# Second chunk's hidden states and first two weight blocks loaded before the last stores of the first phase; its first in-projection ahead of scan unit 0

## The reference, cut to what matters

```python
def _direction(x_bdl, conv_w, conv_b, xproj_w, dtproj_w, dtproj_b, A_log, Dv):
    xc = lax.conv_general_dilated(x_bdl, conv_w, (1,), [(D_CONV - 1, 0)], ...)   # 4 taps, per channel
    xc = (xc + conv_b[None, :, None]).transpose(0, 2, 1)
    x_dbl = xc @ xproj_w.T
    dt = x_dbl[..., :DT_RANK] @ dtproj_w.T + dtproj_b
    Bm = x_dbl[..., DT_RANK:DT_RANK + D_STATE]
    Cm = x_dbl[..., DT_RANK + D_STATE:]
    xc = jnp.clip(xc, -10.0, 10.0)
    dt = jnp.clip(dt, 1e-05, 1.0)
    delta = jax.nn.softplus(dt + dtproj_b)
    A = -jnp.exp(A_log)
    return _selective_scan(xc, delta, A, Bm, Cm, Dv)   # h = exp(delta*A)*h + delta*u*B; y = sum over 16 states of C*h
xz = (hidden_states @ in_proj_w.T).transpose(0, 2, 1)
x, z = jnp.split(xz, 2, axis=1)                        # 2048 channels each
y_fwd = _direction(x, ...)
y_bwd = _direction(x[:, :, ::-1], ...)[:, ::-1, :]
y = (y_fwd + y_bwd) * jax.nn.silu(z.transpose(0, 2, 1))
out = y @ out_proj_w.T
```

## Time and profile before

| | us |
|---|---|
| median of 3 runs | 8235.12 |
| lowest and highest | 8234.53, 8238.75 |
| the profiled execution, whole | 8231.93 |
| its span, first to last instruction | 8230.1 |

### The profile page before, as it was taken

How to read it: one execution, slowest core, us unless ns; L and a number is a source line. 1 busy time by engine, 2 the same in 40 slices (tenths; PEclk the granted TensorE clock), 3 DMA queues, 4 the chain that set the end, 5 groups by cost and what they waited for, 6 DMA issues and landing times. The chain is left out here.

```text
span 8230.1 us, 114768 instructions
## 1 busy us (share of the span) xinstructions
PE 7136.7 (87%) x32512; PEld 4393.1 (53%) x32512; DVE 7156.1 (87%) x7788; ACT 5349.8 (65%) x12640; POOL 6715.8 (82%) x2320
## 2 busy tenths in 40 slices
PE   6578888888888888877899999999999988789999
PEld 3344555555555555554555555555555555534444
DVE  6913999999999999999999999999999999934443
ACT  6634777777777777777777777777777777610000
POOL 5513999999999999999999999999999999821110
PEclk8789999999999999998999999999999999889999
DMA  3363232323232323221323232323233332153442
GB/s 103 90 191 128 70 118 66 118 70 118 67 118 68 119 67 118 68 98 44 113 79 128 76 128 77 131 79 126 89 116 104 104 107 70 63 191 133 136 140 76
DMA packets 557719, 844.05 MB, mean 103 GB/s; under 512 B 129472, under 2 KB 276928, under 8 KB 539712
## 3 DMA queue, kind: packets, MB, share of 16 engines
q1 hardware_dynamic: 557120, 837.10, 31.1%
HBM read 583.89 MB, written 253.02 MB: 102 GB/s over the span
## 5 line engine op out<-in xcount | busy, mean ns | idle before, releaser
L1192 POOL TENSOR_TENSOR scan_w<-scan_du,scan_bcast_b 128x2048 f32<-128x2048 f32 x1023 | 4623.9, 4544 | 45.0 <-DVE scan_h L1239 6.6
L1239 DVE TENSOR_TENSOR_SCAN scan_h<-scan_da,scan_state,scan_w 128x512 f32<-128x512 f32 x2560 | 3185.3, 1276 | 44.2 <-ACT scan_da L1094 27.7
L1094 ACT ACTIVATE scan_da<-scan_delta,scan_prm 128x512 f32<-128x512 f32 x4096 | 2803.1, 685 | 0.0
L973 PE MATMUL scan_yT<-all_ident,scan_hc 128*128 128x128 f32 x10240 | 1540.1, 281 | 660.4 <-DVE scan_hc L1249 659.6
L1239 DVE TENSOR_TENSOR_SCAN scan_hs<-scan_da,scan_state,scan_w 128x512 f32<-128x512 f32 x1536 | 1891.9, 1258 | 45.2 <-ACT scan_da L1094 44.7
L973 PEld LDWEIGHTS scan_yT<-all_ident,scan_hc 128*128 128x128 f32 x10240 | 1175.3, 143 | 1395.5 <-DVE scan_hc L1249 1047.1
L846 PE MATMUL scan_in_ps<-scan_hn,scan_win 128*128 128x512 f32 x3840 | 1732.3, 594 | 13.6 <-issue 13.6
L1249 DVE TENSOR_TENSOR scan_hc<-scan_h,scan_bcast_c 128x512 f32<-128x512 f32 x2560 | 1637.3, 671 | 2.1 <-ACT scan_state L1074 0.7
L1202 POOL TENSOR_TENSOR scan_hp<-scan_hs,scan_bcast_c 128x1024 f32<-128x1024 f32 x512 | 1209.3, 2362 | 49.9 <-DVE scan_hs L1239 42.9
L846 PEld LDWEIGHTS scan_in_ps<-scan_hn,scan_win 128*128 128x128 f32 x3840 | 693.6, 191 | 715.6 <-issue 715.6
L1074 ACT ACTIVATE scan_state<-scan_h 128x1 f32<-128x1 f32 x2560 | 429.5, 168 | 982.8 <-DVE scan_h L1239 977.0
(11 more groups left out here) (122 smaller groups left out, 6918.3 us busy)
## 6 DMA issues: line engine op xcount, KB each, us to landing
yT<-scan_y_out SPq DMA_DIRECT2D x257, 256.0 KB, 2.0
scan_win<-winx SPq DMA_DIRECT2D x128, 512.0 KB, 3.7
xc<-scan_xc_out SPq DMA_DIRECT2D x256, 256.0 KB, 2.0
scan_xc<-xc SPq DMA_DIRECT2D x256, 256.0 KB, 4.1
scan_bcast_b<-bc SPq DMA_DIRECT2D x64, 1024.0 KB, 8.0
scan_bcast_c<-bc SPq DMA_DIRECT2D x64, 1024.0 KB, 8.2
scan_win<-winz SPq DMA_DIRECT2D x128, 512.0 KB, 4.6
scan_x<-x_pad SPq DMA_DIRECT2D x128, 257.5 KB, 2.6
```

The costliest lines, as they stand in the source:

```text
L973: last = nc.tensor.matmul(yT[:, tb], hc_slot(b, n)[:, tb * P:(tb + 1) * P], ident[:], is_transpose=True, start=(i == 0 and tb == 0), stop= ...
L1094: nc.scalar.activation(da[:, n % 2], delta[:, s], ACT.Exp, scale=decay(b, n)).then_inc(S["exp_done"], 1)
L1192: nc.gpsimd.tensor_tensor(w[:, g], du[:].unsqueeze(1).to_broadcast([P, G, T]), bcast_b[:, g * G:(g + 1) * G], ALU.mult).then_inc(S["w_done ...
L1239: nc.vector.tensor_tensor_scan(flip(b, h_slot(b, n)), flip(b, da[:, n % 2]), flip(b, w[:, n // G, n % G]), state_of(b, n), ALU.mult, ALU.a ...
```

## The change

Three things are moved. In SP's order, `load_win(16)`, `load_hn(1)` and `load_win(17)` leave `between` and stand in the last pair of `before_scan`, behind a hold for the last in-projection matmul of the first chunk and in front of the stores of blocks 14 and 15. On PE both halves of the in-projection of block 16 stand in front of unit 0, behind `dt_matmul(0)`, and on ACT its copy stands there too, behind `delta_step(0)`. In unit 0, block 16 has only its convolution and projection left (states 5 and 8), block 17 is projected in at states 0 and 2 instead of 8 and 10, copied at 7 instead of 11, and convolved at 9 instead of 11. The first `turn` of unit 0 moves from state 6 to 8 and its copy and addition to where they are in all units.

```diff
         NORMAL = dict(into=(0, 2), diag=1, copy=7, conv=5, xc=10, proj=11)
-        EARLY = dict(into=(0, 2), diag=1, copy=5, conv=5, xc=8, proj=8)
+        EARLY = dict(into=(), diag=1, copy=NS, conv=5, xc=8, proj=8)
         TURN = dict(diag=1, conv=2, xc=7, proj=8)
-        LATER = dict(into=(8, 10), diag=6, copy=11, conv=11, xc=12, proj=13)
+        LATER = dict(into=(0, 2), diag=6, copy=7, conv=9, xc=12, proj=13)
...
         def turn_steps(b):
-            if b == 0:
-                return dict(mm=(6, 12), copy=(10, NS - 1), add=(12, NS - 1))
             return dict(mm=(8, 12), copy=(12, NS - 1), add=(12, NS - 1))
...
                 store_bc(0)
-                for a in range(2):
-                    load_win(DB + a)
                 hold(sp, S["bc_stored"], LOAD, S["passed"])
                 for c, g in ((0, 0), (0, 1), (1, 0)):
                     broadcast(0, c, g)
-                load_hn(1)
                 load_c_columns(0)
...
                         load_win(a + 2)
+                if j == DB // 2 - 1:
+                    hold(sp, S["in_mm"], DB, S["passed"])
+                    load_win(DB)
+                    load_hn(1)
+                    load_win(DB + 1)
                 for a in (j * 2, j * 2 + 1):
                     before_scan(a)
             between()
...
                 pe.wait_ge(S["scan_done"], b * NS + TN[k] + 1 + SCR)
-                pe.wait_ge(S["in_copied"], (in_copies(b) if b or k else DB + 1) + 2)
+                pe.wait_ge(S["in_copied"], in_copies(b) + 2)
...
                     pe.wait_ge(S["in_copied"], i + 2)
-                    if b or i > DB:
-                        pe.wait_ge(S["h_turn_copied"], b * NTN if b else 1)
+                    if b:
+                        pe.wait_ge(S["h_turn_copied"], b * NTN)
                     in_proj(i % 2, 0, KT // 2)
...
             dt_matmul(0)
+            in_step(DB, 0, 0)
+            in_step(DB, 1, 0)
             for b in range(NU):
                 unit(b)
...
             delta_step(0)
+            act.wait_ge(a_in[DB % 2], (DB // 2 + 1) * (NA * LOAD))
+            in_copy(DB)
             for b in range(NU):
                 unit(b)
```

## The result

| | before | after |
|---|---|---|
| median of 11 runs each, us | 8234.53 | 8216.05 |
| lowest and highest | 8222.72, 8238.75 | 8209.94, 8224.22 |
| ratio, 95% interval | | 0.9982 (0.9974 to 0.9989) |
| profiled execution, whole | 8231.93 | 8214.63 |
| its span | 8230.1 | 8212.9 |

The change gains 18.5 us by the medians, with an interval of 9 to 21 us. The forecast was 15 us, 8220 for the median.

The account below looks back on a forecast made before the run. DVE was taken to bound the units, POOL close behind. Start -6.6, unit 0's idle time +21.0 and unit 1 +0.5 made 15 us, 8235.1 to 8220; forecast 8216.5 to 8224 (0.60), 8 in 10 within 8212 to 8228.

Parts of the forecast that it names:

- rival 1: Last stores of chunk 0 are not held up by the loads; gain 19 us, 8216 us; chance 0.20.
- The store of xc 14 behind the loads: On SP's queue, this store waits for the 3.4 MB asked for ahead; delay 3.8 us (2.3 to 5).
- Columns of C in time: At the start of unit 0, columns arrive near 736, ACT needs them near 738; the 5.04 us wait goes.
- In-projection 16 ahead of unit 0: On PE, 16 matmuls starting at half clock put the first scan at P0 + 12.0; this wait costs 2.8 us.
- P0: The moment PE gets `load_p(0)` and begins `dt_matmul(0)`; 719.21 before, predicted 723.0.
- Unit 0: DVE's first unit: the 8.10 and 8.70 us waits go, idle time falls from 27.3 to 6.3 us.
- DVE's own count: First scan 735.0 + 24.84 + 2.6 for ACT's extra work allows unit 1 at 762.4, sooner than PE's path.
- 3.7 us later at no cost: Slack claimed for the start of unit 0, as PE's path was taken to be later than DVE's count.
- POOL's path: In unit 0, POOL's first weighted pair at P0 + 28.4, then PE, ACT and DVE work: unit 1 at P0 + 42.7.
- The clock's second fall: PE nearly idle from 748 to 751 may drop to half clock; costs 0 to 3 us, 0.4 counted.
- Unit 1: DVE's second unit, 1.3 us over the steady time; keeps about 0.8 of that, gives 0.5 us.
- Rival 3, POOL's lead: POOL no longer runs ahead, and over 0.13 us more in each of some 250 units gives 8252; chance 0.04.

Follow-up runs that it names:

- half of `hn`: The change, with only half of the second chunk's hidden states loaded (1 MB of 2); not timed, dt matmul 2.0 us sooner than the change.
- the weights apart: The change, with block 16's weights loaded one in-projection sooner and block 17's behind the columns of C; not timed, dt matmul 0.9 us sooner.
- the best kernel: The change, with unit 0 and 1 loads first, last four stores and B/C store before one hold, convolution 17 at state 7; 8206.40 us, ratio 0.9968.

## Why the prediction held, step by step

The time lay in the range, the forecast was 3.5 us short of the median's gain and within 0.2 us of the gain at unit 2 (15 and 15.2). The main mechanism held: the loads came early enough for both in-projections, and the long waits went at the price of a later start. That the sum came out so close is partly luck, as its errors offset each other: the start lost 8.3 us for 6.6, the idle time of unit 0 fell by 22.1 for 21.0, and unit 1 gave 1.3 for 0.5. The time alone would even fit rival 1 better (8216, measured 8216.05); only the trace rules it out. Step by step, against the working of the prediction:

- *The store of xc 14 behind the loads.* Right in kind, too small: 3.8 us said (2.3 to 5), 5.2 measured, just outside the bounds. Two terms were mis-sized. The 3.67 MB were to be through at M+11.1, and the traffic ended near M+11.7; 0.8 us were taken from there to the next load, and it took 1.5. The runs with less ahead of the store show that bytes over one rate are not the whole of it: 1 MB less gave 2.4 us at the hold with `hn` and 0.9 to 1.2 with weights. Rival 1 (no delay) is out.
- *Columns of C in time.* Right: asked for at M+25.3, no wait at 736.29.
- *In-projection 16 ahead of unit 0.* First scan at P0 + 12.2, said 12.0 (its own terms add up to 12.3). The clock rose 5.5 us into TensorE's work, and 5.8 to 7.6 us in four more traces that start it at half clock; keeping it busy gave 2.7 us at the first scan, said 2.8 for the whole wait.
- *Unit 0.* It lasted 30.0 us, 31.1 said. The wait at state 13 was named, 3 to 4 us, and measured 2.98. Its cause was mis-stated for the change as it is: not POOL's pair, which ended at 748.65 when TensorE still worked on the products of DVE, but the string of TensorE's work that begins when DVE's products come (747.83, after a wait of 1.83 for them) and ends with the convolution. So in the change the end of unit 0 hangs on the first scan: in the five traces with this schedule of unit 0 and no wait for the pair, it lasts 30.0 us, wherever P0 lies (half of `hn`: P0 2.0 us sooner, first scan and unit 1 only 0.9 to 1.0). The step that was wrong is DVE's own count, 24.84 + 2.6 = 27.4 us from the first scan to unit 1: 30.0 were measured, and the "3.7 us later at no cost" that came of it is not there.
- *POOL's path.* It is real all the same, 0.6 us short of being the late one in the change (748.65 against 749.27, when TensorE had done the products). With DVE's start 2.7 us sooner it took the whole gain back. Unit 1 came at P0 + 42.7 there, the sum of the prediction, but not by its terms: the pair ended at P0 + 27.3, said 28.4 (its terms add up to 28.7), and the work from there to the end of the convolution took 7.4 us for 6.0, as the clock fell. The 2.7 us at the start were free in the sense that winning them alone wins nothing.
- *The clock's second fall.* 0.4 us were put in for it. In the change it didn't happen; in three of the four runs with an earlier start it did behind the pair, and cost 1.6 to 1.7 us there. With the convolution at state 7 there was no gap at that place and the clock stayed full.
- *Unit 1* gave 1.3 us instead of 0.5: all of its short waits went.
- *Rival 3, POOL's lead.* DVE has no idle time in the window of unit 3, POOL's 0.30 us are as before. It didn't happen.

The rest of the difference, 15.2 to 18.5 us, is inside the interval of the measurement.

## What to carry to other kernels

A transfer that a hold waits for paid here for what was asked for ahead of it in the queue (5.3 us for 3.4 MB): before a large load is moved forward, look for the next small one that the critical engine needs, and ask for that first. Where several engines reach the same state late, one wait removed showed the next (columns, block 16, block 17, POOL's pair, `turn`), and an edit that is worth 0.9 us alone can be worth 6 us behind another. Splitting a change into its halves, 6.2 and 1.0 us for 13.8 together, tells more than its total.

## What the runs showed of the hardware

- The queue of SP passed 3.67 MB of mixed loads and stores in about 11 us; with 1 MB less of `hn` the store behind was done 2.4 us sooner, with 1 MB less of weights 0.9 and 1.2 us. In both traces with the weights apart the DMA engines went on for over 2 us after the bulk, at a share of 0.12 and 46 GB/s in the windows shown.
- A gap in TensorE's work cost beyond itself: after two idle stretches of 1.3 us, 12 small turns and 2 projection matmuls took 3.75 us for 2.17, at a granted clock of 0.50. One of 1.83 us in the change, with nothing idle behind it, left the clock at 1.00.
- Without any change to them, the stages ahead of the scan ended between 698 and 709 us in twelve traces. Such a spread hides the 11 us between the best kernel and the change in single runs, and counting from a common moment in the trace brings them out.
